# Attention epilogue: the per-query factor spread over 64 partitions by a matmul and a copy instead of a DMA

## The reference

```python
attn = einsum('bhqd,bhkd->bhqk', q, k) * HD ** -0.5        # 16 heads of 64, T = 2048
attn = where(causal, attn, -inf)
m = max(attn); e = exp(clip(attn) - m)
p = e / (sum(e) + 1e-06);  p = p + 1e-08;  p = p / sum(p)
out = einsum('bhqk,bhkd->bhqd', p, v)                      # -> (B, T, 1024)
x = layernorm(x + out @ w_proj.T)
x = layernorm(x + (gelu((x @ U1) @ V1 + b1) @ U2) @ V2 + b2)
```

## Time and profile before

| | us |
|---|---|
| median of 2 runs | 2054.79 (2049.75 and 2059.83) |
| the profiled execution | 2052.97 |
| its span, slowest core | 2051.4 |
| spans of the 8 cores | 2043.3 to 2051.4 |

### The profile page before, as it was taken

How to read it: one execution, slowest core, us unless ns; L and a number is a source line. 1 busy time by engine, 2 the same in 40 slices (tenths; PEclk the granted TensorE clock), 3 DMA queues, 4 the chain that set the end, 5 groups by cost and what they waited for, 6 DMA issues and landing times.

```text
span 2051.4 us, 15884 instructions; the slowest of 8 cores (2043.3 to 2051.4 us)
## 1 busy us (share of the span) xinstructions
PE 1310.1 (64%) x4376; PEld 438.5 (21%) x4376; DVE 648.4 (32%) x1041; ACT 607.7 (30%) x740; POOL 19.4 (1%) x46
## 2 busy tenths in 40 slices
PE   0698766765766667567576675676666119459962
PEld 0243311211212112112121121121122003123420
DVE  2200055424334234234333342332400035531047
ACT  0122101332333333233233333233244102344660
POOL 0000000000000000000000000000000000000000
PEclk9999965555555555555555555555555559579985
DMA  7500010113022121131221211302312671000003
GB/s 237 172 1 1 0 36 1 6 16 21 3 18 19 5 18 7 15 21 4 17 19 6 19 6 16 21 3 18 16 5 8 168 249 42 0 0 1 0 1 164
DMA packets 28788, 70.83 MB, mean 35 GB/s; under 512 B 3232, under 2 KB 16544, under 8 KB 24096
## 3 DMA queue, kind: packets, MB, share of 16 engines
q10 hardware_dynamic: 5120, 8.39, 11.1%
q1 hardware_dynamic: 20864, 52.52, 7.7%
q0 software_dynamic: 2720, 8.92, 1.8%
HBM read 44.06 MB, written 8.39 MB: 26 GB/s over the span
## 4 chain that ended last, share of the span: by engine, by line
PE 55%; DVE 14%; DMA 12%; ACT 12%; issue 6%; ACTq 1%; DVEq 0%; SPq 0%; PEldq 0%; PEld 0%
PE PS L490 13%; PE PS L525 10%; PE PS L406 8%; DVE mx_sb L436 8%; ACT pt L505 7%; DMA ba_f<-alpha 6%; PE PS L308 5%; PE PS L755 3%; PE PS L327 3%; PE PS L828 3%; PE PS L810 3%; PE PS L417 2%; DVE x_f L723 2%; DVE x_f L719 2%; DMA stgB<-xT 1%
## 5 line engine op out<-in xcount | busy, mean ns | idle before, releaser
L436 DVE TENSOR_REDUCE mx_sb<-PS 128x1 f32<-128x512 f32 (+3 forms) x576 | 359.8, 625 | 413.2 <-PE PS L406 253.4
L490 PE MATMUL PS<-qs,ks 65*128 65x512 bf16 (+3 forms) x640 | 318.9, 549 | 243.2 <-ACT pt L505 221.1
L505 ACT ACTIVATE pt<-PS 128x1024 bf16<-128x1024 f32 (+3 forms) x256 | 241.7, 944 | 606.4 <-PE PS L490 564.1
L406 PE MATMUL PS<-kp,qp 64*128 64x512 bf16 (+3 forms) x640 | 268.6, 522 | 175.8 <-DVE mx_sb L436 164.4
L525 PE MATMUL PS<-pt,vT_all 128*65 128x512 bf16 (+3 forms) x640 | 274.8, 563 | 25.5 <-ACT pt L512 25.5
L490 PEld LDWEIGHTS PS<-qs,ks 65*128 65x128 bf16 x640 | 72.7, 121 | 443.2 <-issue 443.0
L561 DVE TENSOR_TENSOR op<-PS,ba_f 64x512 bf16<-64x512 f32 x64 | 43.7, 683 | 371.5 <-DMA ba_f<-alpha 298.4
L308 PE MATMUL PS<-x_bf,wqk_bf 128*128 128x512 bf16 x512 | 114.6, 385 | 66.7 <-DVE wqk_bf L286 66.7
L406 PEld LDWEIGHTS PS<-kp,qp 64*128 64x128 bf16 x640 | 53.6, 100 | 410.3 <-issue 399.4
L525 PEld LDWEIGHTS PS<-pt,vT_all 128*65 128x65 bf16 x640 | 99.6, 172 | 93.2 <-issue 81.1
L755 PE MATMUL PS<-op,wpot 128*128 128x512 bf16 x256 | 60.4, 392 | 81.2 <-DVE wpot L740 81.2
(11 more groups left out here) (77 smaller groups left out, 810.1 us busy)
## 6 DMA issues: line engine op xcount, KB each, us to landing
stgB<-xT SPq DMA_DIRECT2D x8, 1024.0 KB, 6.8
stgB<-wqkT SPq DMA_DIRECT2D x8, 1024.0 KB, 6.1
ba_f<-alpha ACTq DMA_DIRECT2D x64, 128.0 KB, 6.3
x_f<-xT SPq DMA_DIRECT2D x8, 1024.0 KB, 7.1
out<-x_f SPq DMA_DIRECT2D x8, 1024.0 KB, 3.9
stgD<-U SPq DMA_DIRECT2D x5, 1024.0 KB, 6.9
stgD<-V SPq DMA_DIRECT2D x5, 1024.0 KB, 6.1
qs<-qp POOLq DMA_DIRECT2D x17, 256.0 KB, 7.3
```

Of the source, the lines that this page charges most:

```text
L406: prow=prow: e.matmul(PS0[:, lo:lo + w], q_pairs[p2][prow:prow + 64, 128 * i:128 * i + 128], k_pairs[p2][prow:prow + 64, a:a + w], start=T ...
L436: e.reduce_max(mx_sb[:, xcol:xcol + 1], PS0[:, lo:lo + w], axis=AX.X),
L490: cpos=cpos: e.matmul(PS0[:, lo:lo + w], k_stage[hb][:, 128 * j:128 * j + 128], q_stage[qb4][:, cpos:cpos + w], start=True, stop=True),
L505: e.activation(pt[:, cpos - q0:cpos - q0 + span], PS0[:, 0:span], AF.Exp),
```

## The change

The DMA of stream "ab" goes, with its tile `ba_f32`. In its place `emit_epi_piece` has, between L555 and the multiply, an f32 matmul of a row of ones with alpha into bank 2 + qb % 2 of PS0, which the strips use too, and a DVE copy from there to a new tile `ba_sb` of 512 columns, one for all pieces. The multiply reads that tile.

```diff
-    ba_f32 = alloc(grpC, "ba_f32", [64, T], F32, side="right")
+    ba_sb = alloc(grpC, "ba_sb", [64, 512], F32, side="right")
@@ emit_epi_scalar
-        p.dma("ab", "scalar", lambda e, a=a: e.dma_start(
-            out=ba_f32[:, a:a + 512].unsqueeze(1),
-            in_=alpha[0:1, a:a + 512].unsqueeze(1).broadcast_to([1, 64, 512])),
-            reads=[("alpha", qb)], writes=[("ba", qb)])
@@ emit_epi_piece
+        bank = 2 + qb % 2
+        lo = 512 * bank
         p.op("tensor", lambda e, a=a, h=h: e.matmul(
             PS1[0:64, a:a + 512], vt8_sb[0:1, 65 * h:65 * h + 64],
             u_bf[0:1, a:a + 512],
             start=False, stop=True, skip_group_check=True),
             reads=[("vt8",), ("ubf", qb)], writes=[("P1", qb)])
+        p.op("tensor", lambda e, a=a, lo=lo: e.matmul(
+            PS0[0:64, lo:lo + 512], ones_rowf[0:1, 0:64],
+            alpha[0:1, a:a + 512], start=True, stop=True),
+            reads=[("onrf",), ("alpha", qb)], writes=[("P0", bank)])
+        p.op("vector", lambda e, lo=lo: e.tensor_copy(
+            ba_sb[:, :], PS0[0:64, lo:lo + 512]),
+            reads=[("P0", bank)], writes=[("ba",)])
         p.op("vector", lambda e, a=a, pair=pair, prow=prow:
              e.tensor_mul(O_pairs[pair][prow:prow + 64, a:a + 512],
-                          PS1[0:64, a:a + 512], ba_f32[:, a:a + 512]),
-             reads=[("P1", qb), ("ba", qb)], writes=[("O", pair)])
+                          PS1[0:64, a:a + 512], ba_sb[:, :]),
+             reads=[("P1", qb), ("ba",)], writes=[("O", pair)])
```

## The result

| | before | after |
|---|---|---|
| median of the runs, us | 2054.1 (10 runs) | 2077.2 (11 runs) |
| ratio after to before | | 1.0114, 95% interval 1.0079 to 1.0148 |
| attention stage, mean of the 8 cores, us | 1266.0 | 1290.1 |

The changed kernel is 1.1% slower: 23 us by the medians, within 2%, on the slower side. The attention stage (first DMA of the row maxima to first DMA of x_f32, by the chains of the eight cores) took 24.1 us more, so nothing is left over for other stages. The profiled execution of after has its slowest core, core 2, at 2086.8 us; its matmuls of the FFN ran at a granted clock of 0.91, those of core 5 at 1.00, and core 5 ended at 2073.8.

The account below looks back on a forecast made before the run. Bound: mostly PE work (57% of a pair's chain) with ACT and DVE round trips. Costs 10.1 minus wins 5.3 gave +4.8 a pair, +33.6 for seven, -0.4 and -4.4 for the last heads: +28.8 on 2053.0, 2082 us; range 2070 to 2092.

Parts of the forecast that it names:

- The cost of the matmul: New f32 matmul in each epilogue piece: PE free again 1.70 us after its start, its end at 1.91.
- The copy: DVE copy from PSUM before the multiply: 0.68 us taken from multiply L561, left open between 0.43 and 0.77.
- The wait of the strips for the bank: Strip matmul wanting the new matmul's PS0 bank waits for the copy; L406 behind piece 0 about 1.1 us.
- S + 2.83: Start of a strip matmul wanting the same PS0 bank, 2.83 us after the new matmul's start S.
- The size of the slots: PE's spacing in a piece: u matmul L555 takes 0.56 us, the f32 matmul behind it 1.70.
- The ends of the heads: DMA stalls removed: exp 3.54 us earlier at even ends, reductions 3.64 at odd; 2.62 and 2.72 net of piece 3.
- The last pair and the end: Heads 14 and 15, without strips, and the stage's very end: -0.4 and -4.4 us.
- The rival of hidden waits: PE's waits for DVE in later strips hide the copy wait; a pair nets about 0, 2050 us, chance 0.12.
- The signs named beforehand: After-profile: L406 waits about 1.1 us, copy 0.68, head-end waits gone with PE below 1.5, pair 169 for 164.
- three signs of being wrong: Pair at 164 us or less, copy far from 0.68, or attention stage's granted clock above 0.55.
- The rival of the dearer matmul: Weight load of 0.33 us not hidden between bf16 matmuls: 21 us more at most, 2103, chance 0.14.
- The clock: Rival: closed PE gaps raise the attention stage's clock, 0.21 us back per upper-level microsecond; 2009 with 350 more; chance 0.05.

Follow-up runs that it names:

- a2_ownbank: Changed kernel with the f32 product written to partitions 64 to 127 of the piece's own PS1 bank, not a PS0 strip bank; 2035.8 us, ratio 0.9911.
- a9_cols: Changed kernel with the f32 product written to partitions 64 to 127 of the same PS0 strip bank, not 0 to 63; 2051.9 us, ratio 0.9995.
- a7_both: Changed kernel with the product in partitions 64 to 127 of PS1, plus alpha in bf16 and a bf16 matmul; 1969.4 us, ratio 0.9578.

## Why the prediction was right, point by point

The forecast was +28.8 us; the attention stage took +24.1 (eight cores) and the medians differ by 23. The way and the mechanism were right: the DMA's two stalls went, and the new matmul and copy cost more than that in the places where the DMA had been hidden. The size came out 5 us too high. Time from one u matmul to the next, core 5, mean of the seven pairs (the last column of six), from the starts in the timelines, against the steps of the sum:

| from, to | before | after | measured | forecast |
|---|---|---|---|---|
| piece 0 to 1, even head | 15.52 | 17.88 | +2.36 | +2.83 |
| 1 to 2, even | 7.08 | 8.57 | +1.48 | +2.29 - 0.60 = +1.69 |
| 2 to 3, end of even head | 8.55 | 5.24 | -3.31 | -3.54 + 0.60 = -2.94 |
| 3 to 0 of the odd head | 45.90 | 47.06 | +1.16 | +0.92 |
| 0 to 1, odd | 17.04 | 19.54 | +2.50 | +2.2 |
| 1 to 2, odd | 6.73 | 8.65 | +1.92 | +2.8 - 0.6 = +2.2 |
| 2 to 3, end of odd head | 18.73 | 15.70 | -3.03 | -3.64 + 0.60 = -3.04 |
| 3 to 0 of the next pair | 43.87 | 45.13 | +1.25 | +0.92 |
| sum | | | +4.34 | +4.78 |

- **The cost of the matmul** (1.70 a piece, on the path): right. It shows as two records with an end after 1.91 us, and doubling it cost 1.65 each.
- **The copy** (0.68, after the multiply's row): 683 ns. The low bound of 0.43 did not come. This agrees with the rule of the Trainium skill on PSUM operands (VectorE: DVE Perf Modes, "Why PSUM operands drop a tier").
- **The wait of the strips for the bank**: 0.94 and 0.39 us. S + 2.83 was forecast, S + 2.84 measured (894.72 to 897.56).
- **The size of the slots**: the sum put the f32 matmul 0.56 behind the u matmul, where L406 had stood, and the next one 1.70 behind it. They come 0.43 and 1.84 behind (912.44, 912.87, 914.71). For PE that is the same, 2.27 for 2.26; but the copy starts 0.13 earlier, and each of the places that wait for it costs so much less: at the lower clock piece 0 of the even head takes 2.69 in place of 2.83 (15.46 to 18.15 us in most pairs). With four or five such places a pair this is worth 0.5 to 0.7. Two other steps erred the other way: by the medians of the seven pairs, which leave most upper-clock stretches out, piece 0 of the odd head cost 2.85 (forecast 2.2, the middle between 1.8 at the upper clock and 2.7 at the lower) and piece 3 of the even head 1.16 (forecast 0.92). The medians of all eight steps sum to +4.86. The seven pairs took 29.1 us more on core 5 (forecast 33.6), while seven times that sum is 34: what was missing lies in stretches at the upper clock and not in the steps at the lower one. So single steps were off by up to 0.65, and that they offset one another to within 0.1 in the sum of the medians is partly luck.
- **The ends of the heads**: right to 0.01 at the odd head's end in the mean, but by the medians 3.28 were won, so the 0.01 is chance. At the even one the mean won 0.37 more; in two of the seven pairs of core 5 an upper-clock stretch lay on it (4.17 us in place of 5.61), and the other five won 2.88 in the mean, for a forecast of 2.94.
- **The last pair and the end**: forecast -4.8. From the last DMA of the row maxima to the first of x_f32 it is 118.96 us in place of 124.91 on core 5, -5.95; over the six cores whose chain shows both ends in both profiles the mean is -4.0.
- **The rival of hidden waits** (2050) fell: the wait for the copy and PE's time both count.
- **The signs named beforehand**: PE's wait for the copy behind piece 0 is 0.94 (1.1 was named), its wait at the even head's end 1.54 (under 1.5), a pair takes 167 us (169), and none of the three signs of being wrong came.
- **The rival of the dearer matmul** (2103) fell: u matmul, f32 matmul and the next slot take 2.27 together, where 2.26 were forecast, so no weight load of 0.33 holds PE.
- **The clock**: the granted clock of the attention stage is 0.51 before and after:

```profile
340.00:1634.00 1294.00, 939.71 (x2520) 270.56 (x2520) 455.80 (x859) 414.33 (x584) 13.70 (x27) 0.51 0.02 6
```

PE is busy 939.71 of 1294 us for 828.64 of 1272, its gaps of 6 us are closed, and the clock did not rise. Upper-clock time fell, from 41 to 27 us a core in the mean of the eight (windows of 1 us). By the estimate of 0.21 us given back for each microsecond, those 14 us are worth 3. With bf16 in place of f32 the mean was 36, but in `a2_ownbank`, with the same f32 matmuls, it was 40. So the f32 matmuls alone do not explain the fall, and its cause is not shown.

Where the gain went: the forecast had the two ends win 3.54 + 3.64 = 7.2 us a pair, and they won 3.31 + 3.03 in the rows of the table and some 0.6 each in the row ahead, where the DMA's issue is gone (ACT's idle of 0.71 between alpha and the next exp is 0.01 after): 7.5. The change paid for them in four places of a pair where the DMA had cost nothing, and once more in pieces 3.

## What to carry to other kernels

A DMA that is issued early and waited for late cost nothing here in four of eight places; read in the timeline where it is waited for, and put a price on the replacement in all the places. On an engine that carries the path, new work counts nearly in full (here 1.65 of 1.70 us a matmul), except where a wait for another engine follows at once, as in pieces 3. Before moving a small product to another engine, look for output partitions that leave it beside the matmul in front, and for a bank that nobody else wants.

## What the runs showed of the hardware

- Two matmuls whose outputs lie in partitions 0 to 63 and 64 to 127 started at the same time (717.79 both in `a2_ownbank`, in one bank; 676.20 both in `a9_cols`, in two banks), and in `a7_both` the bf16 one of 512 columns then added nothing to PE's sequence. In `a9_cols`, which changed nothing else, this was worth 25 us, 0.4 us a piece.
- A DMA that spreads one partition's 2 KB over 64 partitions took 6.3 us to land (128 KB), over 16 partitions 2.7 us (32 KB). Two together took up to 12.3 us, and 4 KB issued 0.9 us behind one, from another queue, took 5.6 in place of 1.65.
- An f32 matmul of 512 columns behind the bf16 u matmul started 0.43 us after it, where a bf16 strip matmul had started after 0.56; a bf16 matmul behind the f32 one came 1.84 after it, an f32 one 1.70 (705.78 behind 704.08).
